# A graph network's softmax attention layer: each eight row gathers wait for the landing of the eight before the last, instead of the last eight

## The reference, cut to what matters

```python
h = (x @ W_att).reshape(n, H, D)
a_src = jnp.einsum('nhc,hc->nh', h, att_src)
a_dst = jnp.einsum('nhc,hc->nh', h, att_dst)
e = a_src[src] + a_dst[dst]
e = jnp.where(e > 0, e, SLOPE * e)
m = jax.ops.segment_max(e, dst, num_segments=n)
e = jnp.exp(e - m[dst])
s = jax.ops.segment_sum(e, dst, num_segments=n)
msg = (e / (s[dst] + SM_EPS))[:, :, None] * h[src]
out = jax.ops.segment_sum(msg, dst, num_segments=n)
```

## Time and profile before

| | |
|---|---|
| three runs | 5760.69, 5765.54, 5777.83 us; median 5765.54 |
| span of the profiled execution | 5738.2 us |
| that execution's own time | not listed apart from the runs; the median is 27.3 us over the span |
| share of the span busy | TensorE 58%, VectorE 62%, ScalarE 38%, GpSimd 39% |
| first and last start of the gathers of L1711 | 4080.4 and 5298.7 us |
| last sums of the layer (L1905) | 5535.9 us |

### The profile page before, as it was taken

One profiled execution on the slowest core, in us unless ns is written; L12 is line 12 of the kernel. 1 busy time (PEld: TensorE's weight loads), 2 busy tenths in 40 slices (PEclk: granted clock), 3 DMA queues, 4 the chain that ended last, 5 costly groups with the idle time before them and its releaser, 6 DMA issues. The chain is left out here.

```text
span 5738.2 us, 59061 instructions
## 1 busy us (share of the span) xinstructions
PE 3339.7 (58%) x14332; PEld 2164.9 (38%) x14332; DVE 3535.7 (62%) x6569; ACT 2184.6 (38%) x3989; POOL 2244.9 (39%) x2086
## 2 busy tenths in 40 slices
PE   5666679999999999798413433325014342433564
PEld 3555534444444444355312323324013232323452
DVE  6999989999999999510214323325135553645676
ACT  4999968887878787300000000000002111111310
POOL 0000023333333333100276777773566666666200
PEclk8999989999999999899655555555555555555556
DMA  2555544444444443697411242210211111111011
GB/s 71 163 163 162 162 134 118 114 118 108 124 104 114 119 109 100 134 195 157 93 37 39 47 90 50 47 45 18 36 28 36 31 36 30 35 31 29 5 38 35
DMA packets 546254, 474.36 MB, mean 83 GB/s; under 512 B 185773, under 2 KB 439736, under 8 KB 545085
## 3 DMA queue, kind: packets, MB, share of 16 engines
q1 hardware_dynamic: 493723, 416.13, 28.6%
q0 software_dynamic: 52288, 55.34, 4.8%
HBM read 351.39 MB, written 119.84 MB: 82 GB/s over the span
## 5 line engine op out<-in xcount | busy, mean ns | idle before, releaser
L813 PE MATMUL l_sum_ps<-arena,sums 125*65 125x500 f32 (+1 forms) x2600 | 1140.8, 577 | 9.9 <-ACT arena L774 4.8
L1711 POOL DMA_INDIRECT l_rows<-table,tile_src x782 | 794.4, 1016 | 406.9 <-issue 212.0
L1126 POOL DMA_INDIRECT l_rows<-hidden_rows,tile_src x782 | 796.3, 1018 | 326.4 <-issue 231.8
L692 POOL COPY arena<-arena 125x750 f32<-125x750 f32 (+1 forms) x400 | 540.4, 1355 | 893.8 <-PE l_count_ps L802 855.7
L758 ACT ACTIVATE arena<-arena,far_left 125x750 f32<-125x750 f32 (+1 forms) x800 | 713.4, 939 | 282.7 <-DVE arena L711 282.7
L711 DVE SCALAR_TENSOR_TENSOR arena<-arena,far_past 125x750 f32<-125x750 f32 (+1 forms) x800 | 803.8, 1045 | 16.5 <-DMA arena<-score_rows 16.5
L722 DVE SCALAR_TENSOR_TENSOR arena<-arena,l_count_ps 125x750 f32<-125x750 f32 (+1 forms) x800 | 735.4, 960 | 96.5 <-ACT arena L763 51.9
L1187 PE MATMUL l_sum_ps<-l_rows,l_hot 128*125 x1612 | 359.9, 414 | 747.0 <-issue 678.7
L1153 DVE TENSOR_TENSOR sums<-sums,l_sum_ps 125x64 f32 x806 | 178.5, 222 | 744.4 <-DMA arena<-counts 527.5
L1187 PEld LDWEIGHTS l_sum_ps<-l_rows,l_hot 128*125 128x125 f32 x1612 | 341.3, 323 | 765.9 <-issue 765.3
L763 ACT ACTIVATE arena<-arena 125x1500 f32<-125x1500 f32 (+1 forms) x400 | 596.1, 1491 | 0.0
(11 more groups left out here) (438 smaller groups left out, 3032.3 us busy)
## 6 DMA issues: line engine op xcount, KB each, us to landing
arena<-counts SPq DMA_DIRECT2D x300, 328.1 KB
counts<-arena SPq DMA_DIRECT2D x324, 284.4 KB
arena<-counts SPq DMA_DIRECT2D x21, 2843.8 KB
arena<-counts SPq DMA_DIRECT2D x100, 382.8 KB
l_attr<-edge_attr_in SPq DMA_DIRECT2D x97, 256.0 KB
arena<-score_rows SPq DMA_DIRECT2D x24, 732.4 KB
l_rows<-hidden_rows,tile_src POOLq DMA_INDIRECT x782
l_rows<-table,tile_src POOLq DMA_INDIRECT x782
```

The lines of the kernel that those rows point to most:

```text
L692: g.tensor_copy(laid[k % 2][:, 0:n * P].rearrange("p (b v d) -> p b v d", b=n, d=D), raw[k % RAWS][:, 0:n * P].rearrange("p (v b d) -> p b ...
L813: last = nc.tensor.matmul(sum_ps[0:F + 1, c, 0:hi - lo], h_one[:, w, :], z[k % ZS][:, lo:hi], start=(w == 0), stop=(w == W - 1))
L1126: pool.indirect_dma_start(rows[:, b % RING, t, :], None, m.hidden_rows[:, :], bass.IndirectOffsetOnAxis(ap=m.tile_src[:, k:k + 1], axis=0) ...
L1711: pool.indirect_dma_start(rows[:, t % RING3, :], None, m.table3[:, :], bass.IndirectOffsetOnAxis(ap=m.tile_src[:, t:t + 1], axis=0)).then_ ...
```

## The change

```diff
@@ -1706,8 +1706,8 @@
                         tile_firsts(p, firsts_in)
                 if t >= RING3 and t % 8 == 0:
                     pool.wait_ge(sums_ready, (t + 7 - RING3 + NW - 1) // STEPS + 1)
-                if t and t % U == 0:
-                    pool.wait_ge(*landed(t // U - 1))
+                if t >= 2 * U and t % U == 0:
+                    pool.wait_ge(*landed(t // U - 2))
                 pool.indirect_dma_start(rows[:, t % RING3, :], None, m.table3[:, :],
                                         bass.IndirectOffsetOnAxis(ap=m.tile_src[:, t:t + 1], axis=0)
                                         ).then_inc(rows_in[t // U % RING], 16)
```

## The result

| | before | after |
|---|---|---|
| runs | 5760.69 to 5777.83 us, median 5769.51 of 4 | 5850.47, 5858.38, 5886.15, 5894.72 us, median 5872.26 |
| ratio | | 1.0183, 95% interval 1.0159 to 1.0207 |
| span of the profiled execution | 5738.2 us | 5848.7 us (its own time 5850.47) |
| gathers of L1711, first and last start | 4080.4 to 5298.7 us | 4093.8 to 5411.4 us |

5632.5 us was forecast. The kernel became 103 us slower and not 133 faster.

A forecast was written before the change was run, and what follows sets the result against it. GpSimd's gathers were taken to set the pace of parts 0 to 11. Savings of 54.7 + 104.2 - 23.1 = 135.8 us, less 3 for stretching, gave 5765.5 - 133 = 5632.5 us, range 5598 to 5668 us.

The forecast's parts named there:

- What bounds the kernel: GpSimd's L1711 gathers set the pace of parts 0 to 11; TensorE waits for rows, 552.7 us in 12 waits.
- The turns: TensorE's turn_far points, one per part: 100.6 us apart before, forecast 89.0 us apart after the change.
- One head in each cycle is held by the gate: GpSimd's wait for TensorE's sums stops one batch's first gather per later cycle: 3.3 us each, 23.1 us in all.
- The sum: Whole kernel: 54.7 + 104.2 - 23.1 = 135.8 us saved, less 3 for stretched gathers: 133 us.
- Heads of 0.30 us: Gap before a batch's first L1711 gather falls to 0.30 us, from 1.74 in the first 320 tiles, 2.16 later.
- the cost of two satisfied waits: At a batch's first gather, two satisfied waits were taken to cost nothing visible; the other end was 0.42 us more.
- A rule beside it: Skill page's fixed 2.0 us per GpSimd transfer: 0.85 us saved per batch start, 80 us in all, about 5686 us.
- 5609 and 5653: Forecast's own bounds in us: sums never stop GpSimd (23 less); satisfied waits still cost 0.42 us at 49 batch starts (21).
- queues and other engines: Behind GpSimd's waits stand only its gathers; VectorE isn't held up; some 3 us more stretching of gathers.
- The slower rival: L1711 gathers behind the first batch take longer beside others in flight: at worst 6461 us; chance 0.03.
- the first rival: GpSimd's wait for TensorE's sums replaces the landing wait; only the first 39 batches gain, 54.7 us, 5711 us; chance 0.06.
- The 27.3 us around the span: Runs' median over the profiled span of 5738.2 us, added unchanged to the forecast.

The follow-up runs named there:

- free sessions: Sessions in which the kernel before took 5623 to 5634 us and no profile showed other engines delayed beside GpSimd's gathers.
- e15: The changed kernel, unaltered, run again in a session where the kernel before took 5634.03 us: 5499.43 us, ratio 0.9764.
- e4_tilesum: The kernel before with a landing wait added in the earlier layer, tile_sum, ahead of each eight gathers: 5766.42 us, ratio 1.0259 where nothing was held up.
- held-up session: A session in which the kernel before took 5754 to 5770 us and every profile showed other engines delayed beside GpSimd's gathers.
- session 1: The first measurement of the changed kernel against the kernel before: before's median 5769.5 us, ratio 1.0183.

## Why the prediction was wrong

**What bounds the kernel: right, for free sessions only.** There each term can be compared. The turns of e15 lie (5059.57 - 4527.72) / 6 = 88.6 us apart, 89.0 was forecast. One head in each cycle is held by the gate, for 3.0 to 3.2 us, 15.0 us after the turn (4631.45 - 4616.44); 3.3 and about 14.9 were forecast. TensorE's wait ahead of a turn is 29.6 us, about 27 was forecast. From `turn_far(11)` to `turn_far(12)` there are 58.6 us (5118.18 - 5059.57); 59 was forecast. The median of L1711 is 955 ns. The sum was 133 us, and 134.6 were measured, in a kernel that starts from another time. That isn't luck: e4_tilesum has attend3 as in before, in a free session. Its gathers start over 1219.4 us (4136.2 to 5355.6) and e15's over 1083.4 (3997.5 to 5080.9), 136.0 less, and before's over 1218.3 in the held-up session that the sum was read from.

**Heads of 0.30 us: right in both kinds**, and the cost of two satisfied waits was nothing. The 80 us of "A rule beside it" are outside of what either kind shows. One sum of the prediction doesn't come out: 5609 and 5653 with 12 us at both ends are 5597 to 5665, and not 5598 to 5668. It changes nothing.

**The step that failed** is the part on queues and other engines: "VectorE itself isn't held up: the scan of L1755 takes 2.28 us beside gathers and 2.28 after their end", together with "What stands behind GpSimd's waits is only its own gathers". The evidence was of the wrong sort. It compares how long an instruction takes, and the hold-up isn't in instructions but in the ends of waits and in what the sequencer does. In the trace of before it stood open, in four places. First, VectorE idled 744.4 us ahead of L1153 in tile_sum, and I took from that layer only that its gathers went out well. Second, the view of L1952 in the trace of before has this row:

```profile
L1952 ACTq FUSED_REGOPS  x1263: 3/64/1395, 4199.8 to 5440.0; - x181
```

Its longest is 1395 ns, where e15's is 175. Third, the wait of 12.84 us ahead of `turn_far(4)` next to one of 38.50 ahead of `turn_far(5)` meant that TensorE had needed 83 us for the one cycle and 62 for the next, with the same work. I noted it ("by a microsecond or two") and didn't ask why. In e4_tilesum, free and with the same attend3, that wait is 37.78 us:

```profile
4630.39 1.90 PE L1871 MATMUL l_far_ps<-ident,l_rows 128*64 128x128 f32 x8 [37.78 <-DMA l_rows<-table,tile_src]
```

Fourth, beside the 32 gathers of L1716, from 5376.5 us on, TensorE gets 15.87 us of work done in 42, and in e15, beside the same gathers, 37.61 in 43 (before first, then e15, in the columns of the earlier trace rows):

```profile
5376.00:5418.00 42.00, 15.87 (x62) 13.69 (x61) 11.26 (x32) 7.10 (x34) 32.04 (x32) 0.50 0.06 6
5159.00:5202.00 43.00, 37.61 (x155) 34.12 (x154) 34.32 (x101) 22.28 (x124) 33.54 (x32) 0.50 0.07 6
```

**The slower rival had the right sign and the wrong mechanism.** I looked for a price on the gathers themselves. They kept their 952 ns at the median; the price fell on everybody else. VectorE's idle time ahead of the accumulation rose by 600.8 - 221.2 = 380 us, and TensorE's wait for rows, which had been the cover for such things, fell by 552.7 - 182.2 = 370 us: it was used up. The stretch of L1711 became 1317.6 us long (5411.4 - 4093.8) after 1218.3 in before, where e15 has 5080.9 - 3997.5 = 1083.4, and my sum had 1218.3 - 133 = 1085.

**The gate took its place** as in the first rival, but only as a consequence. GpSimd ran ahead while the sums crawled, then stood for 161.9 us, and later for up to 16.1 us at once. In the free session the same gate costs 26.3 us in all.

**The 27.3 us around the span** were no time around the span. The changed kernel's profiled execution has a span of 5848.7 us and took 5850.47: 1.8 us lie around it. I had compared one execution's span with the median of others.

## What to carry to other kernels

A wait that looks like the bottleneck of one engine can be what protects the others, as this one did in held-up sessions. Before taking it away, look in the same trace for a stretch where the thing that it paces already runs without a pause, and read there the idle time of all the other engines, whether waits end when what they wait for is done, and the durations of the sequencers' instructions, not only those of the operations. And measure such a change in more than one session: here its sign depended on it.

## What was not expected of the hardware

**Back-to-back gathers from GpSimd hold up the other three engines, in some sessions.** In session 1 waits ended 17 us late, register instructions of ScalarE took 0.70 us in place of 0.064, and the same part took 302 us in place of 60. The Trainium skill, page "SBUF — State Buffer", section "SBUF: two separate sides", says that DMA and compute operations can't slow each other down. The durations of operations agree (281 or 282 ns at the mean for L1826 in every profile), so what is held up lies outside of what that rule covers.

**It comes and goes.** Four sessions had it and two had not, with no session between, and the same chip 6 had it once and once not. Before differs by 120 to 147 us, the changed kernel by 356 to 373 (5855.78 to 5872.26 against 5499.43). Of before's difference 71 us lie in tile_sum (above) and some 32 behind `turn_far(12)`: from there to the last sums of L1905 it takes 200.1 us (5535.9 - 5335.8), and e15 167.7 (5285.9 - 5118.2). Between them, in attend3's gathers, there is none, for TensorE's waits for rows take the hold-up in.

**What stays open.** Neither the path on which waits and register instructions are delayed nor what makes a session held-up is settled, and no run looked at what else was at work on the chip. Whether it is the issuing of gathers on GpSimd or their transfer that delays the others isn't told apart either. Slower packets are not the cause. In a stretch with back-to-back gathers, 4240 to 4300 us, the packets of the gathers' queue took 18.6% of the 16 engines' time in the held-up profile after and 17.0% in the free e15, which for each packet is within 3%. Here are that queue's rows and those of the one for instructions (packets, MB, share), after first:

```profile
q0 software_dynamic: 1528, 1.80, 18.6%
q14 instruction: 2, 0.02, 0.1%
```
```profile
q0 software_dynamic: 1435, 1.68, 17.0%
q14 instruction: 2, 0.02, 0.1%
```

A rival that no run tests is that the engines wait for their own instructions. Against it speaks only that this queue's packets are as few in one kind as in the other.
